# Self- and cross-attention of a decoder layer: row maxima for four heads at a time, and the scores of two heads in separate halves of TensorE's rows

## The chip, the cores and the metric

The kernel runs on one core of a Trainium2 chip (trn2). The metric is device time in microseconds, the median of three executions: 1087.91 us before the change (1082.69 to 1088.86).

## The reference, cut to what matters

One decoder layer over x (2 x 1024 x 256, float32) and a context (2 x 77 x 256): a causal self-attention block with a recurrent scan and an MLP behind it, a cross-attention block, and a tree-routed feed-forward. Both attentions have 16 heads of 16 features. What the change touches:

```python
# self-attention, b=2, h=16, 1024 queries and keys, 16 features
scores = jnp.einsum('bhqd,bhkd->bhqk', q, k) / np.sqrt(HD).astype(np.float32)
scores = jnp.where(causal[None, None], -jnp.inf, scores)
attn_w = jax.nn.softmax(scores, axis=-1)
attn = jnp.einsum('bhqk,bhkd->bhqd', attn_w, v)
...
# cross-attention: the same over 77 keys, without the mask
scores = jnp.einsum('bhsd,bhtd->bhst', qh, kh) / jnp.sqrt(jnp.float32(D_K))
attn = jax.nn.softmax(scores, axis=-1)
```

## The kernel before

The layer is one program with an instruction stream written out by hand for each engine. Semaphores set the order between engines; within an engine the order is that of the code. The attention stages, which run from about 89 to 398 us (self) and from about 726 to 826 us (cross), are the same code with an object `A` (`SA` or `XA`).

**Quads.** The 16 heads x 2 batches are taken as 8 quads of four heads, n = 2 * it + qd, on two sets of buffers (qd = 0, 1). q and k of a quad are first written to DRAM, each as a rounded high part and a low part, and are loaded back by SP in the two layouts below.

**First pass, the maxima (PE `unit`, DVE `maximum`).** It uses q1 and k1, the high parts alone: four heads of 16 features are interleaved on 64 partitions (the other 64 are zero), and k1 holds for each head a copy in which the other heads' rows are zero. One unit is one head h, one tile i of 128 queries and up to 512 keys: a matmul of 128, 256, 384 or 512 columns into bank 5, 6 or 7 of PSUM (`nbanks` is 3). Where it reaches the diagonal, a second matmul of 128 columns adds the mask: ident_b (128 x 128) as the weights, causal_b as the columns. A quad has 48 units, 32 of them with a mask. DVE reduces each to one column of part_max (128 x 64), `gather` reduces that to row_max (128 x 32), PE transposes it (`turn`), DVE negates it into neg_max, and SP copies neg_max by DMA into q2 (`load_max`).

**Second pass, the probabilities (PE `scores`, ACT, POOL, PE `weigh`).** The scores are computed transposed, with keys as the output's partitions, and the query's negated maximum is added by the matmul itself: q2 and k2 hold three parts of each head's 16 features (R2 = 48 rows) and one row for the maximum. Two heads (j = 0, 1) share one q2 of 98 rows: head 0 on rows 0 to 47, head 1 on rows 48 to 95, the maxima on rows 96 and 97. k2 has one copy for each j in which the other head's 48 rows are zero, so each of the two matmuls runs over all rows of the array. A quad has 12 steps (a chunk c of 512 queries by a tile kt of 128 keys; at the diagonal 512, 384, 256 or 128 columns), each with two pairs p. One ACT instruction takes exp of a pair (128 x 1024), POOL zeroes the upper triangle of the diagonal block, and `weigh` multiplies by the values with four heads side by side in 32 columns of the array each, 8 matmuls in plain float32.

**Order on PE.** While it computes quad n's second pass, PE works ahead on quad n + 1's first pass (and the first 8 units of n + 2). In a step: `scores` p = 0, a quarter of the step's units, `scores` p = 1, a quarter, `weigh` of the step before, then the other half of the units. `A.plan` deals the units to steps by their columns. A unit waits until DVE has reduced the unit three before it (`s1_free`), `scores` waits for the exp that read its banks (`prob_ready`), `weigh` for exp and for POOL's mask. In the last quad there are no units left.

**Order on SP.** For each quad: `load_first` (q1, k1), `load_second` (q2, k2: three DMAs), stores and loads of results, `load_max`. During the first quad's units, `qk_beside` puts the projections of the second batch between them (one at every third unit from u = 6), and SP stores those.

**POOL at the start (`preset_keys`, `preset_rest`).** It writes the zeros and ones of k1, k2, q1, q2, once for each attention stage, with a tensor_scalar of 10.8 us on two rows twice for SA.

## Time and profile before

| what | before |
|---|---|
| median of 3 (us) | 1087.91 (1082.69 to 1088.86) |
| the profiled execution's own time (us) | 1090.43 |
| its span, first to last instruction (us) | 1088.9 |
| busy share: PE / DVE / ACT / POOL | 85% / 59% / 43% / 16% |
| instructions | 13085 |
| first pass: L1395 matmuls / L1398 masks / L1051 reduces | 384 / 256 / 384 |
| second pass, self: L1421 / L1439 matmuls, L758 exps | 384 / 768 / 192 |
| mean granted TensorE clock, share of full | 0.914 |
| HBM traffic over the span | 72 GB/s |

Times are microseconds from the first instruction of one profiled execution, unless marked ns. A PE matmul's time runs from its start to the modelled end of its pipeline, so matmuls that follow one another overlap: the pace of a stream is read from their starts, or from the time of a merged group. PEld is the load of a matmul's weights. "PEclk" is the granted TensorE clock as a share of 2.4 GHz. A line number names a line of the kernel before; where the printed code is a helper, the tile's names tell whose instruction it is.

### The profile page before, as it was taken

To read this page: it belongs to the slowest core of one execution; us is meant where nothing else is said; L and a number is where in the kernel's file an instruction comes from. 1 tells how busy PE (TensorE), PEld (TensorE's weight loads), DVE (VectorE), ACT (ScalarE), POOL (GpSimd) and SP (SyncE) were. 2 spreads that over 40 slices of the span, in tenths; PEclk is the share of its full clock that TensorE was granted. 3 is DMA by queue.
4 is the path that set the end of the run, shared out by engine and by line. 5 is a ranking of instruction groups with operands and counts; after the bars stand their busy time and mean duration, and the time that the engine had idled before them with its cause. 6 is when DMAs were issued, how large, how long until landed. Compare 5 with 4: busy or idle time off the path is not lost. (4 is left out here: it accounts for less than half of the span.)

```text
span 1088.9 us, 13085 instructions
## 1 busy us (share of the span) xinstructions
PE 930.5 (85%) x4200; PEld 569.7 (52%) x4200; DVE 639.8 (59%) x1023; ACT 465.8 (43%) x683; POOL 170.0 (16%) x200
## 2 busy tenths in 40 slices
PE   5767699999999986999997899954673899999996
PEld 3553455555555433544445778622230477777774
DVE  4635677777777415277785644433331667777775
ACT  2301055555655662466654455412542243333332
POOL 7910012211122212000011400200010001111110
PEclk9887699999999997899998899975876889999998
DMA  3056534323444115100000000055854000000002
GB/s 119 19 201 179 192 78 108 98 67 75 105 108 98 33 59 198 70 1 0 1 0 23 2 1 1 2 180 161 234 154 130 21 0 20 20 19 19 19 20 77
DMA packets 34329, 79.34 MB, mean 73 GB/s; under 512 B 8121, under 2 KB 11193, under 8 KB 33897
## 3 DMA queue, kind: packets, MB, share of 16 engines
q1 hardware_dynamic: 29288, 70.64, 22.1%
q10 hardware_dynamic: 2688, 5.33, 1.4%
q0 software_dynamic: 2304, 2.76, 1.0%
q8 instruction: 27, 0.44, 0.2%
q14 instruction: 22, 0.17, 0.1%
HBM read 48.34 MB, written 30.10 MB: 72 GB/s over the span
## 5 line engine op out<-in xcount | busy, mean ns | idle before, releaser
L1051 DVE TENSOR_REDUCE part_max<-psum 128x1 f32<-128x512 f32 (+3 forms) x384 | 197.5, 553 | 85.5 <-PE psum L1398 54.9
L758 ACT ACTIVATE prob<-psum 128x1024 f32<-128x1024 f32 (+1 forms) x192 | 145.8, 809 | 107.9 <-PE psum L1421 107.8
L1395 PE MATMUL psum<-k,q 128*128 128x512 f32 (+3 forms) x384 | 141.3, 418 | 22.4 <-DMA k<-k 16.7
L1395 PEld LDWEIGHTS psum<-k,q 128*128 128x128 f32 x384 | 73.8, 202 | 88.3 <-DVE part_max L1051 60.5
L1421 PE MATMUL psum<-q,k 128*128 128x512 f32 (+3 forms) x384 | 105.7, 373 | 7.5 <-DMA q<-neg_max 6.2
L652 POOL TENSOR_SCALAR_AFFINE_SELECT prob<-prob 128x256 f32<-128x256 f32 x128 | 52.1, 416 | 256.9 <-ACT prob L758 255.7
L915 ACT ACTIVATE silu<-psum,wt 128x512 f32<-128x512 f32 x64 | 40.5, 685 | 117.2 <-DVE decide L1294 86.0
L1439 PE MATMUL psum<-prob,vq 128*32 128x512 f32 (+3 forms) x768 | 81.8, 498 | 2.0 <-POOL prob L652 1.6
L1421 PEld LDWEIGHTS psum<-q,k 128*128 128x128 f32 x384 | 61.4, 196 | 21.0 <-ACT prob L758 9.9
L1305 DVE TENSOR_TENSOR masked_lo<-masked,masked_hi 128x1024 fp32r<-128x1024 f32 x32 | 47.0, 1468 | 38.5 <-ACT masked_hi L923 38.5
L328 PE MATMUL psum<-masked_hi,wt_hi 128*128 128x512 f32 x128 | 56.1, 438 | 6.6 <-DVE res L1310 6.4
L1398 PE MATMUL psum<-causal_b,ident_b 128*128 128x128 bf16 x256 | 60.7, 239 | 0.0
L1525 PE MATMUL psum<-act_u,wx 128*128 128x512 f32 x128 | 55.8, 593 | 0.0
L1525 PE MATMUL psum<-nrm,wx 128*128 128x512 f32 x128 | 55.6, 593 | 0.0
L1401 PE MATMUL psum<-xk,xq 128*128 128x312 f32 (+1 forms) x64 | 24.8, 438 | 34.3 <-DVE row_max L1054 17.9
L758 ACT ACTIVATE xprob<-psum 77x1024 f32<-77x1024 f32 x32 | 31.6, 1014 | 49.2 <-PE psum L1421 49.1
L328 PE MATMUL psum<-tree_hi,wt_hi 128*128 128x512 f32 x128 | 51.3, 401 | 0.2 <-ACT silu L915 0.2
L330 PE MATMUL psum<-masked_hi,wt_lo 128*128 128x512 f32 x128 | 51.2, 400 | 0.0
L329 PE MATMUL psum<-masked_lo,wt_hi 128*128 128x512 f32 x128 | 51.2, 400 | 0.0
L329 PE MATMUL psum<-nrm_lo,wt_hi 128*128 128x512 f32 x128 | 50.9, 398 | 0.0
L330 PE MATMUL psum<-tree_hi,wt_lo 128*128 128x512 f32 x128 | 50.8, 397 | 0.0
L1054 DVE TENSOR_REDUCE row_max<-psum 128x4 f32<-128x312 f32 x64 | 28.9, 477 | 32.5 <-PE psum L1401 31.6
(165 smaller groups left out, 1656.4 us busy)
## 6 DMA issues: line engine op xcount, KB each, us to landing
q<-q SPq DMA_DIRECT2D x8, 768.0 KB, 6.3
k<-k SPq DMA_DIRECT2D x16, 384.0 KB, 8.4
xq<-xq SPq DMA_DIRECT2D x8, 768.0 KB, 5.6
wt<-in_wt SPq DMA_DIRECT2D x8, 513.0 KB, 3.7
q<-part_hi SPq DMA_DIRECT2D x16, 256.0 KB
k<-part_hi SPq DMA_DIRECT2D x16, 256.0 KB
o<-stage SPq DMA_DIRECT2D x8, 512.0 KB, 7.7
xq<-xpart_hi SPq DMA_DIRECT2D x16, 256.0 KB
```

The source lines that it names most:

```text
L328: pe.matmul(out, rounded(w_hi), rounded(x_hi), start=start, stop=False)
L329: pe.matmul(out, rounded(w_hi), rounded(x_lo), start=False, stop=False)
L330: return pe.matmul(out, rounded(w_lo), rounded(x_hi), start=False, stop=stop)
L652: pool.affine_select(out=blk, in_=blk, compare_op=ALU.is_ge, fill=0.0, base=0, pattern=[[0, 2], [1, P]], channel_multiplier=-1)\
L758: act.activation(A.prob[0:A.keys, s % 2, p, :, q0:CH], psum[0:A.keys, 2 * p:2 * p + 2, q0:CH], ACT.Exp, scale=SCALE)\
L1051: dve.tensor_reduce(part_max[:, at:at + 1], psum[:, 5 + u % A.nbanks, 0:nk], AX_X, ALU.max)\
L1305: dve.tensor_tensor(rounded(masked_lo[:, st.buf]), masked[:, st.buf], masked_hi[:, st.buf], ALU.subtract)\
L1395: mm = pe.matmul(psum[:, 5 + u % A.nbanks, 0:nk], A.q1[:, qd, i * P:(i + 1) * P], A.k1[:, qd, h, k0:k0 + nk], start=True, stop=not diag)
L1398: mm = pe.matmul(psum[:, 5 + u % A.nbanks, nk - P:nk], ident_b[:], causal_b[:], start=False, stop=True)
L1421: mm = pe.matmul(psum[0:A.keys, 2 * p + j, q0:CH], A.k2[:, qd, p, j, kt * P:kt * P + A.keys], A.q2[:, qd, p, c * CH + q0:(c + 1) * CH], st ...
L1439: mm = pe.matmul(psum[32 * h:32 * h + 32, 4, q0:CH], A.vq[:, qd, kt, h, :], A.prob[:, s % 2, h // 2, h % 2, q0:CH], start=first, stop=last)
L1525: mm = pe.matmul(bank(2 * c + m), wx01[:, k, m * P:(m + 1) * P], state(n)[:, k, cols_of(c)], start=False, stop=k == 1, skip_group_check=True)
```

## The change

- **Units.** A unit is now a tile i of queries by one tile kt of 128 keys for all four heads: always 4 x 128 = 512 columns, 36 units a quad, over 64 rows instead of 128. The 8 diagonal units get their mask by two matmuls of 256 columns (causal_b, now 64 rows x 2, as the weights; a 64 x 64 identity repeated for four heads as the columns). DVE reduces 512 columns to four maxima in one instruction, as it did in cross-attention; part_max grows to 32 x 8 columns, which `gather` reduces.
- **Scores.** The heads of a pair lie on partitions 0 to 48 and 64 to 112: 48 rows of features and one of the maximum (q2) or of ones (k2) each. The matmul of head j reads those 49 rows alone. k2 has lost its copies with zeros. q2 is loaded by two DMAs instead of one (`ld2_n` 16 * 4).
- **Presets.** The zeros of q1 and q2, the full zeroing of k2 and POOL's tensor_scalar are gone.
- `weigh`, exp, POOL's mask, the order on PE and the number of banks stay as they are. Both attention stages take part in the scores' and the presets' change; the new units are self-attention's.

```diff
+HALF = P // 2
-        ident_b = sb("ident_b", [P, P], BF16)
-        causal_b = sb("causal_b", [P, P], BF16)
+        ident_b = sb("ident_b", [HALF, 1, HALF], BF16)
+        causal_b = sb("causal_b", [HALF, 2, P], BF16)
-        part_max = sb("part_max", [P, 64])
+        part_max = sb("part_max", [P, 32, SEQ // P])
-        k2 = sb("k2", [P, 2, 2, 2, SEQ], F32R, s_self)
+        k2 = sb("k2", [P, 2, 2, SEQ], F32R, s_self)
...
-        self_units = [(h, i, kh * CH, min(CH, (i + 1) * P - kh * CH), i // TPC == kh)
-                      for h in range(4) for i in range(SEQ // P) for kh in range(i // TPC + 1)]
+        self_units = [(kt, i, kt * P, CH, i == kt) for i in range(SEQ // P) for kt in range(i + 1)]
...
-                sp.dma_start(A.q2[0:2 * R2, qd, :, :].bitcast(F32),
-                             A.q3[4 * qd:4 * qd + 4, :, :, at].rearrange("(p j) r d t -> (j r d) p t", p=2))\
-                    .then_inc(A.ld2[qd], 16)
                 for j in range(2):
-                    sp.dma_start(A.k2[R2 * j:R2 * j + R2, qd, :, j, :].bitcast(F32),
+                    sp.dma_start(A.q2[HALF * j:HALF * j + R2, qd, :, :].bitcast(F32),
+                                 A.q3[4 * qd + j:4 * qd + 4:2, :, :, at].rearrange("p r d t -> (r d) p t"))\
+                        .then_inc(A.ld2[qd], 16)
+                for j in range(2):
+                    sp.dma_start(A.k2[HALF * j:HALF * j + R2, qd, :, :].bitcast(F32),
...
-                sp.dma_start(A.q2[2 * R2:2 * R2 + 2, qd, :, :].bitcast(F32), neg_max[:, qd, :].bitcast(F32))\
+                sp.dma_start(A.q2[R2:P:HALF, qd, :, :].bitcast(F32), neg_max[:, qd, :].bitcast(F32))\
...
-                pool.memset(k1[:].bitcast(F32), 0.0)
-                pool.memset(k2[:].bitcast(F32), 0.0).then_inc(zeros_set, 1)
-                pool.memset(k2[2 * R2:2 * R2 + 2].bitcast(F32), 1.0).then_inc(ones_set, 1)
-                for j in range(2):
-                    row = k2[2 * R2:2 * R2 + 2, :, :, j, :].rearrange("r b p n -> r (b p) n")
-                    pool.tensor_scalar(row, row.bitcast(F32), ident[2 * R2:2 * R2 + 2, 2 * R2 + j:2 * R2 + j + 1],
-                                       None, ALU.mult).then_inc(ones_set, 1)
+                pool.memset(k1[0:HALF].bitcast(F32), 0.0).then_inc(ones_set, 1)
+                pool.memset(k2[32:HALF].bitcast(F32), 1.0)
+                pool.memset(k2[HALF + 32:P].bitcast(F32), 1.0).then_inc(zeros_set, 1)
...
-                        dve.tensor_reduce(part_max[:, at:at + 1], psum[:, 5 + u % A.nbanks, 0:nk], AX_X, ALU.max)\
+                        dve.tensor_reduce(part_max[:].rearrange("q (j p i) k -> q p j i k", j=2, p=2)[:, :, :, i, kt],
+                                          heads, AX_X, ALU.max).then_inc(A.s1_free, 1)
...
-                        mm = pe.matmul(psum[:, 5 + u % A.nbanks, 0:nk], A.q1[:, qd, i * P:(i + 1) * P],
-                                       A.k1[:, qd, h, k0:k0 + nk], start=True, stop=not diag)
+                        mm = pe.matmul(heads, A.q1[0:HALF, qd, i * P:(i + 1) * P], A.k1[0:HALF, qd, :, k0:k0 + P],
+                                       start=True, stop=not diag)
                         if diag:
-                            mm = pe.matmul(psum[:, 5 + u % A.nbanks, nk - P:nk], ident_b[:], causal_b[:], start=False, stop=True)
+                            for r in range(2):
+                                mm = pe.matmul(heads[:, :, r * HALF:(r + 1) * HALF], causal_b[:, r, :],
+                                               ident_b[:].to_broadcast([HALF, 4, HALF]), start=False, stop=r == 1)
...
-                                       A.k2[:, qd, p, j, kt * P:kt * P + A.keys],
-                                       A.q2[:, qd, p, c * CH + q0:(c + 1) * CH], start=True, stop=True)
+                                       A.k2[HALF * j:HALF * j + R2 + 1, qd, p, kt * P:kt * P + A.keys],
+                                       A.q2[HALF * j:HALF * j + R2 + 1, qd, p, c * CH + q0:(c + 1) * CH],
+                                       start=True, stop=True)
```

## Rows read from the trace of the kernel before

**Rows 1.** Stretches: length, each engine's busy time, PEclk, DMA share, GB/s

```profile
89.00:134.80 45.80, 37.19 (x127) 20.53 (x128) 33.58 (x66) 5.50 (x8) 0.00 (x0) 0.76 0.63 200
202.60:236.60 34.00, 33.00 (x225) 18.56 (x221) 25.06 (x51) 18.67 (x26) 6.79 (x17) 1.00 0.35 87
...
372.90:398.20 25.30, 22.37 (x153) 9.23 (x153) 2.57 (x2) 18.91 (x26) 7.65 (x17) 1.00 0.17 54
754.00:780.00 26.00, 24.38 (x120) 11.13 (x120) 14.44 (x33) 18.80 (x26) 0.83 (x1) 0.92 0.81 204
```

**Rows 2.** Timeline: DVE's gather of two quads in a row (start, duration)

```profile
335.48 0.22 DVE L1063 TENSOR_REDUCE row_max<-part_max 128x32 f32<-128x64 f32 x1
...
369.30 0.22 DVE L1063 TENSOR_REDUCE row_max<-part_max 128x32 f32<-128x64 f32 x1
```

**Rows 3.** Waits, 134 to 373 us: total, times, longest

```profile
ACT prob L758 <- PE psum L1421: 102.0, 83, 2.7
...
DVE part_max L1051 <- PE psum L1398: 35.9, 70, 0.9
```

**Rows 4.** Timeline of one full step in steady state

```profile
217.19 0.71 PE L1421 MATMUL psum<-q,k 128*128 128x512 f32 x2
...
218.25 1.44 DVE L1051 TENSOR_REDUCE part_max<-psum 128x1 f32<-128x512 f32 x2 [0.27 <-PE psum L1398]
...
218.56 0.40 PE L1395 MATMUL psum<-k,q 128*128 128x512 f32 x1
...
218.89 1.07 PE L1439 MATMUL psum<-prob,vq 128*32 128x512 f32 x8
219.88 0.19 PEld L1395 LDWEIGHTS psum<-k,q 128*128 128x128 f32 x1 [0.84 <-DVE part_max L1051]
...
220.56 0.48 PE L1421 MATMUL psum<-q,k 128*128 128x512 f32 x1
```

**Rows 5.** Chain that ended last: 512-column rounded matmuls at either clock

```profile
1045.72 0.24 PE psum L329
...
1077.12 0.43 PE psum L329
```

**Rows 6.** Timeline of PE in groups of four scores matmuls

```profile
371.22 0.67 PE L1421 MATMUL psum<-q,k 128*128 128x128 f32 x4
...
386.96 1.19 PE L1421 MATMUL psum<-q,k 128*128 128x512 f32 x4
...
389.08 1.38 PE L1421 MATMUL psum<-q,k 128*128 128x512 f32 x4
```

**Rows 7.** Instruction groups by form: count, busy us, mean ns, idle before

```profile
L1051 DVE TENSOR_REDUCE part_max<-psum 128x1 f32<-128x512 f32 x192 | 128.6, 687 | 39.1 <-PE psum L1395 27.4 <-PE psum L1398 10.2
...
L1421 PE MATMUL psum<-q,k 128*128 128x512 f32 x192 | 65.9, 428 | 6.9 <-DMA q<-neg_max 6.2 <-ACT prob L758 0.5 <-issue 0.3
...
L1054 DVE TENSOR_REDUCE row_max<-psum 128x4 f32<-128x312 f32 x64 | 28.9, 477 | 32.5 <-PE psum L1401 31.6
...
L1421 PE MATMUL psum<-q,k 128*128 128x128 f32 x64 | 9.8, 276 | 0.0
...
L1063 DVE TENSOR_REDUCE row_max<-part_max 128x32 f32<-128x64 f32 x8 | 1.8, 220 | 0.8
```

**Rows 8.** Timeline: the first quad's maxima and the start of its second pass

```profile
125.21 1.08 SPq L506 DMA_DIRECT2D q<-neg_max  x1
...
134.81 1.19 PE L1421 MATMUL psum<-q,k 128*128 128x512 f32 x2 [6.17 <-DMA q<-neg_max]
...
135.01 1.28 ACT L758 ACT_TABLE_LOAD   x1 [22.67 <-DMA k<-part_hi]
```

**Rows 9.** Timeline: plain float32 projections, two instructions to a matmul

```profile
44.32 14.16 PE L1355 MATMUL psum<-nrm,w 128*128 128x512 f32 x32
```

**Rows 10.** Timeline: POOL's last preset and the first load behind it

```profile
53.98 3.51 POOL L614 MEMSET q<- 32x4096 f32 x1
...
84.05 0.63 SPq L479 DMA_DIRECT2D q<-q  x1
```

More of the change, by code:

```diff
@@ L266, in __init__ @@
                 self.ld1_n = 16 * 5 if causal else 16
-                self.ld2_n = 16 * 3
+                self.ld2_n = 16 * 4
                 self.nsteps = len(self.steps)
@@ L619, in _ @@
             pool.wait_ge(c_in, 16 * 4)
-            pool.tensor_copy(ident_b[:], ident[:])
+            pool.tensor_copy(ident_b[:, 0, :], ident[0:HALF, 0:HALF])
             pool.tensor_copy(causal_b[:], caus_f[:])
             preset_keys(k1, k2, 1)
-            preset_rest(q1, q2, vq, sums, 1)
+            preset_rest(vq, sums, 1)
             def attention(A, vals, ready):
@@ L688, in _ @@
             pool.wait_ge(xk_st, 16 * 3 * KT)
-            preset_rest(xq1, xq2, xvq, xsums, 2, xprob)
+            preset_rest(xvq, xsums, 2, xprob)
             attention(XA, xvals, (xv_done, 2))
@@ L697, in _ @@
         def _(act):
-            for t, n in ((vec[:], "vec"), (ident[:], "ident"), (caus_f[:], "causal"), (mean_w[:], "mean_w")):
+            for t, n in ((vec[:], "vec"), (ident[:], "ident"), (mean_w[:], "mean_w")):
                 act.dma_start(t, a[n]).then_inc(c_in, 16)
+            act.dma_start(caus_f[:], a["causal"].rearrange("(h r) n -> r h n", h=2)).then_inc(c_in, 16)
             act.dma_start(vbias[:], a["vbias"]).then_inc(w_in3, 16)
@@ L1043, in maximum @@
                     n = 2 * it + qd
-                    h, i, k0, nk, diag = A.units[u]
-                    row = 16 * (h % 2) + 8 * (h // 2) + i
+                    kt, i, k0, nk, diag = A.units[u]
+                    heads = psum[:, 5 + u % A.nbanks, 0:nk].rearrange("q (p j k) -> q p j k", p=2, j=2)
                     dve.wait_ge(A.s1_ps, n * A.nunits + u + 1)
@@ L1049, in maximum @@
                     if A.causal:
-                        at = 2 * row + k0 // CH
-                        dve.tensor_reduce(part_max[:, at:at + 1], psum[:, 5 + u % A.nbanks, 0:nk], AX_X, ALU.max)\
-                            .then_inc(A.s1_free, 1)
+                        dve.tensor_reduce(part_max[:].rearrange("q (j p i) k -> q p j i k", j=2, p=2)[:, :, :, i, kt],
+                                          heads, AX_X, ALU.max).then_inc(A.s1_free, 1)
                     else:
                         dve.tensor_reduce(row_max[:].rearrange("q (j p i) -> q p j i", j=2, p=2)[:, :, :, i],
-                                          psum[:, 5 + u % A.nbanks, 0:nk].rearrange("q (p j k) -> q p j k", p=2, j=2),
-                                          AX_X, ALU.max).then_inc(A.s1_free, 1)
+                                          heads, AX_X, ALU.max).then_inc(A.s1_free, 1)
                 def gather(it, qd):
@@ L1387, in unit @@
                     n = 2 * it + qd
-                    h, i, k0, nk, diag = A.units[u]
+                    kt, i, k0, nk, diag = A.units[u]
+                    heads = psum[:, 5 + u % A.nbanks, 0:nk].rearrange("q (h k) -> q h k", h=4)
                     if u == 0:
@@ L1394, in unit @@
                     if A.causal:
-                        mm = pe.matmul(psum[:, 5 + u % A.nbanks, 0:nk], A.q1[:, qd, i * P:(i + 1) * P],
-                                       A.k1[:, qd, h, k0:k0 + nk], start=True, stop=not diag)
+                        mm = pe.matmul(heads, A.q1[0:HALF, qd, i * P:(i + 1) * P], A.k1[0:HALF, qd, :, k0:k0 + P],
+                                       start=True, stop=not diag)
                         if diag:
-                            mm = pe.matmul(psum[:, 5 + u % A.nbanks, nk - P:nk], ident_b[:], causal_b[:], start=False, stop=True)
+                            for r in range(2):
+                                mm = pe.matmul(heads[:, :, r * HALF:(r + 1) * HALF], causal_b[:, r, :],
+                                               ident_b[:].to_broadcast([HALF, 4, HALF]), start=False, stop=r == 1)
                     else:
                         pe.sem_inc(passed, 1)
-                        mm = pe.matmul(psum[:, 5 + u % A.nbanks, 0:nk].rearrange("q (h k) -> q h k", h=4),
-                                       A.q1[:, qd, i * P:(i + 1) * P], A.k1[:, qd, :, bass.ds(it * CTXP, CTXP)],
+                        mm = pe.matmul(heads,
+                                       A.q1[0:HALF, qd, i * P:(i + 1) * P], A.k1[0:HALF, qd, :, bass.ds(it * CTXP, CTXP)],
                                        start=True, stop=True)
@@ L1691 @@
         "ident": np.eye(P, dtype=np.float32),
-        "causal": np.where(k <= q, 0.0, LOW).astype(np.float32),
+        "causal": np.where(q <= k, 0.0, LOW).astype(np.float32),
         "mean_w": np.full((P, P), 1.0 / D, np.float32),
```

20 lines of the change are left out of this document (8 added, 12 removed).

## The prediction

> **What bounds the kernel now.** I read the page's busy shares first, which say only that PE leads with 85% over a program of many stages, and then the table of stretches, one line to a quad of self-attention. In steady state a quad's second pass lasts 34.0 us, with PE marked busy for 33.0, DVE for 25.1 and ACT for 18.7, all at the full clock [rows 1]. The gathers of neighbouring quads stand 33.8 us apart [rows 2]. Seven quads carry units for later quads; the eighth has none left and takes 25.3 us [rows 1]. These seven are where this change acts, 7 x 34 = 238 us.
>
> Busy PE is not proof, since ends of matmuls are modelled. So I added up PE's own pace. A rounded 512-column matmul follows the next every 0.24 us [rows 5]; four of 128 columns take 0.67 us of which one's own 0.276 is latency, so (0.67 - 0.28) / 3 = 0.13 us each [rows 6, 7]; 384 and 256 columns I put between them at 0.20 and 0.17. One `weigh` of 512 columns holds PE from 218.89 to 219.88, 0.99 us [rows 4]. A quad has, for the scores, 24 matmuls of 512 columns and 8 each of 384, 256 and 128: 24 x 0.24 + 8 x 0.50 = 9.8 us. Its 48 units have the same mixture of columns: 9.8 us. 32 masks of 128 columns at 0.13 are 4.2. The 12 `weigh` are six full ones, 5.9, and two each at three quarters, a half and a quarter of that, 3.0: 8.9. Together 32.7 of the 34.0 us. PE's instruction stream is the bound; DVE and ACT wait for it. The waits agree: ACT stood 102 us for scores and DVE 36 us for masked units, over seven quads [rows 3]. In one full step (217.19 to 220.56, 3.37 us) DVE had two units of work, 1.44 us, and then stood until PE was through `weigh` [rows 4].
>
> **The units.** Columns stay 18,432 a quad, and the masks' 4,096. What goes is small instructions: 36 units x 0.24 = 8.6 us and 16 masks of 256 columns x 0.17 = 2.7, together 11.3 instead of 14.0. That is 2.7 us of PE per quad. From below: if masks in fact hid behind the loads of weights and cost only their columns (4,096 at 0.24 / 512 = 1.9 us before and after), the gain is 9.8 - 8.6 = 1.2 us. Half the rows make a matmul neither shorter nor longer in this sum, since its price goes by columns.
>
> DVE gets 36 reduces of 512 columns. The old ones took 687 ns [rows 7]; the form with four outputs exists in cross-attention, 477 ns for 312 columns, and 200 more at the slope of these two rows, (687 - 477) / 200 = 1.05 ns, meet at 687 ns. So four outputs cost nothing, and 36 x 0.687 = 24.7 us. The gather reads 256 columns instead of 64: 192 x 1.05 ns = 0.20 us on top of 0.22 [rows 7], in the chain gather, `turn`, negate, `load_max`, where it delays a DMA needed some microseconds later. With negate and the reciprocal DVE needs 24.7 + 1.0 = 25.7 us a quad, as now.
>
> **The scores in two halves.** No row of before shows two matmuls in two row halves. Bounds: if they take turns, a pair of 512 columns costs 0.48 us as now; if they run together, 0.24. The nearest row is `weigh`, which puts four heads in four column groups: its eight float32 matmuls take 0.99 us, while such float32 instructions alone follow one another every 14.16 / 32 = 0.44 us [rows 4, 9], so eight in turn would be 3.5 us. The array does work on separate parts at the same time here. I take the near end, with a little for the second head's weights, which go through one load path: 0.28 us for a pair of 512 columns, 0.25, 0.22 and 0.20 for the shorter. 12 x 0.28 + 4 x 0.67 = 6.1 us instead of 9.8: 3.7 us of PE a quad (best case 24 pairs at single price, 4.9; worst 0).
>
> The Trainium skill (TensorE: Matmul & The Clock Gate, section on packing small matmuls) has matmuls in different row groups start about 4 ns apart; by that the pair costs the single price and the gain is the best case. No trace here shows it.
>
> **What the quad becomes.** PE: 34.0 - 2.7 - 3.7 = 27.6 us. DVE at 25.7 is then nearly as long, and the two are tied by three banks: PE may be three units ahead, 3 x 0.687 = 2.06 us, and between units come a `weigh` (0.99) and up to two pairs. That covers most gaps, not all, and each unit's result takes some 0.4 us to arrive (0.40 for one in [rows 4]). I let DVE stand 0.1 us for each of 36 units: 25.7 + 3.6 = 29.3 us, between the floor of 27.6 and the 31.3 of the rival below. Gain 4.7 x 7 = 32.9 us.
>
> **The last quad.** There a full step is 2.12 us (386.96 to 389.08) [rows 6] and ACT's two exps are about 1.94 of it. The scores' gain of 0.4 a step is cut by ACT to about 0.2 to 0.3: 6 full steps x 0.25 and 6 short ones x 0.15 give 2.4 us (bounds 0 and 3.7).
>
> **Before steady state.** From 89 to 124 us the first quad's units run between the projections. PE's second pass starts at 134.81, when the row of maxima has landed that was issued at 125.21 behind the stores of q and k; ACT is free at 135.01 when the last of these stores lands [rows 8]. DVE is busy for 33.6 us there [rows 1]. Every third unit is now 0.69 long instead of 0.51 on average, so the projections spread out by about 0.5 us each, up to 3 us at the last of them, but the DMA queue behind them carries 200 GB/s and is still draining 10 us later. 12 fewer units take the time back for the maxima. I take 0, between -2 and +3 us.
>
> **Presets and DMAs.** POOL ends its presets at 57.5 us and the first load that needs them is issued at 84.05 [rows 10]. Work of up to 30 us goes and gains nothing, since SP's stores of q and k cover it. Without that cover it would have been worth the lot. The same holds in front of cross-attention. One more DMA a quad costs SP about 0.6 us of issue, where SP waits for maxima anyway; bytes are the same.
>
> **Cross-attention.** Its steady part has PE 24.4 of 26.0 us busy, ACT 18.8 and DMA engines at 81% [rows 1]. 32 pairs could save 0.2 each, 6.4 us; most goes to ACT and the loads. I take 1 us (0 to 4).
>
> **Sum.** 32.9 + 2.4 + 0 + 1 = 36.3 us. The span becomes 1088.9 - 36.3 = 1052.6, the profiled execution's own time (1090.43, 1.5 above its span) 1054.1; the median before is 2.5 below that own time, so the same gain gives 1087.9 - 36.3 = 1051.6. I say 1052 us. Its own range is 1040 to 1062: the two PE terms at their better bounds with DVE's standing halved, or the units at their lower bound.
>
> **Rivals.**
>
> *DVE takes over.* PE runs ahead, but DVE's idle time falls only from 8.9 us (34.0 - 25.1) to 6 because units still come in bunches after `weigh`: quad 25.3 + 6 = 31.3, gain 2.7 x 7 + 3 = 22 us, 1066 us. For it: DVE already has 74% of the quad, and a reduce never gets shorter here. Against: in this trace DVE waits for PE, not the reverse. The Trainium skill (TensorEngine Tiling, PSUM Bottleneck) warns of just this: tiling speeds up TensorE but not the emptying of PSUM. Its rule has no figure to add.
>
> *The halves take turns.* Only the units gain, 2.7 x 7 and nothing else, some of it blurred: 1070 us.
>
> *The halves cost a drain.* PE went from a unit at 218.56 (0.24 long) to `weigh` at 218.89: 0.09 us lost at a change of shape [rows 4]. If each pair paid that once or twice, 24 pairs cost 2.2 to 4.3 us a quad against the 2.7 of the units: 1084 us, no change to measure. The skill (TensorEngine Tiling, Key Properties) says that a change of mode drains and a change of tile does not; by it units, masks and scores now share one mode, and the count of changes around `weigh` is as before.
>
> *The clock falls; the slower side.* With 64 and 49 rows in use and PE waiting more, the granted clock could drop in self-attention, where it is 1.00 now. It is 0.76 on average from 89 to 134.8 us, where PE waits for DVE and DMA [rows 1]. At half clock a 512-column matmul paces 0.43 [rows 5] instead of 0.24; a quad's 27.6 us of PE holds some 21 us of streaming, which would double. The gain of 4.7 us is used up when 4.7 / 21 = 22% of the streaming is at half clock. At half of it a quad takes 29.3 + 10.5 = 39.8: 5.8 x 7 = 41 us slower, 1129 us. Against: in the last quad, where PE is 22.4 of 25.3 us busy with gaps of its own, the clock stayed 1.00.
>
> **Chances.** 1052: 0.60. DVE takes over: 0.14. Turns: 0.09. Drain: 0.06. Clock: 0.11, of which 0.10 slower. 0.5% is 5.4 us, about what a measurement of this kernel can tell from no change. Faster 0.84, same 0.06, slower 0.10. The range reaches from the likeliest case's lower end to the two middle rivals: 1036 to 1076 us.
>
> **What would show it.** Second matmul of a pair starting 0.1 us or less after the first, not 0.24. Gathers about 29 us apart. 288 reduces near 687 ns. DVE's waits for units below 20 us in all. Full steps of the last quad near 2.0 us. PEclk 1.00 from 145 to 390 us. It is wrong if pairs start 0.24 apart, if PEclk shows falls there, or if gathers stand over 31 us apart.

## The result, and the profile after

The kernel after takes **1125.01 us** (1117.51 to 1128.56, four runs) against 1085.66 for the kernel before in the same series: ratio **1.034**, interval 1.030 to 1.038. It is slower, by 3.4%. The forecast was 1052 us. Here and in the experiments, medians count all runs, while a ratio and its interval leave out runs more than 1.5% above the fastest of the same kernel, which show a lower granted clock.

The span of its profiled execution is 1123.2 us, 34.3 longer than before. First, where the 34.3 us arose, by four landmarks. The first quad's gather starts at 127.20 us, 3.3 later than before (123.92). From the first gather to the eighth pass 264.2 us instead of 245.4: 18.8 more. From there to the end of the last self-attention `weigh` it is 33.1 instead of 28.9 us: 4.2 more. Between the first and last exp of cross-attention lie 79 us instead of 72: 7 more. The rest comes to about 1 us in sum. None of these four parts became shorter.

The table of stretches, from each gather to the next (length; busy PE, PEld, DVE, ACT, POOL with their counts; PEclk; DMA share; GB/s):

```profile
127.20:172.28 45.08, 38.20 (x154) 18.09 (x154) 24.65 (x40) 16.84 (x20) 3.64 (x10) 0.55 0.38 97
172.28:201.09 28.81, 27.76 (x198) 13.02 (x197) 23.34 (x38) 18.91 (x26) 6.86 (x18) 1.00 0.46 102
201.09:236.46 35.37, 30.45 (x197) 13.91 (x196) 23.94 (x39) 19.02 (x26) 7.34 (x18) 0.89 0.38 84
236.46:285.11 48.65, 48.65 (x205) 21.49 (x197) 24.84 (x38) 19.33 (x26) 6.89 (x17) 0.50 0.32 72
285.11:328.93 43.82, 43.82 (x206) 19.70 (x198) 24.71 (x40) 19.33 (x26) 6.59 (x17) 0.59 0.32 67
328.93:357.46 28.53, 27.73 (x198) 13.02 (x197) 23.35 (x39) 18.91 (x26) 6.91 (x18) 1.00 0.49 104
```

These lines answer to [rows 1, 2]. Two quads ran at full clock throughout: 28.8 and 28.5 us, PE busy for 27.8 and 27.7 of them. The forecast had 29.3 and 27.6. One quad ran at half clock throughout: 48.65 us, PE busy for all of it, DVE and ACT busy for nearly as long as in the fast ones (24.8 and 19.3 us against 23.3 and 18.9). The work in the lines is the same: as many matmuls, reduces and exps. So at half clock a gain of 5 us a quad is a loss of 15. Over the seven quads together (127.20 to 391.42) PEclk is 0.74, against 0.97 from 123.92 to 369.30 in the kernel before: about half of the time is at half clock.

The groups of the page (mean of one, then the idle time before them):

```profile
L1044 DVE TENSOR_REDUCE part_max<-psum 128x4 f32<-128x512 f32 x288 | 185.3, 686 | 112.6 <-PE psum L1388 72.1
L1388 PE MATMUL psum<-k,q 64*128 64x512 f32 x288 | 144.2, 543 | 28.0 <-DMA k<-k 16.8
L1416 PE MATMUL psum<-q,k 49*128 49x512 f32 (+3 forms) x384 | 119.1, 473 | 8.2 <-ACTq L739 6.3
```

288 reduces of four maxima at 686 ns, as forecast. Means of PE (543, 473 ns) mix both clocks.

The timeline of PE at full clock shows the halves at work:

```profile
219.35 0.50 PE L1416 MATMUL psum<-q,k 49*128 49x512 f32 x2
...
221.01 0.49 PE L1388 MATMUL psum<-k,q 64*128 64x512 f32 x1
221.02 0.49 PE L1416 MATMUL psum<-q,k 49*128 49x512 f32 x1
221.34 0.39 PE L1388 MATMUL psum<-k,q 64*128 64x512 f32 x1
221.57 0.59 PE L1416 MATMUL psum<-q,k 49*128 49x512 f32 x2
221.81 0.39 PE L1388 MATMUL psum<-k,q 64*128 64x512 f32 x1
222.04 0.40 PE L1416 MATMUL psum<-q,k 49*128 49x512 f32 x1
222.29 0.49 PE L1388 MATMUL psum<-k,q 64*128 64x512 f32 x1
```

Three units and four score matmuls take 1.28 us, from 221.01 to 222.29; one after another they would take 7 x 0.24 = 1.68. A score matmul, the second head's by its place in the order, begins at 221.02, 0.01 us after a unit in the lower half. The two of a pair take 0.50 us together at 219.35, where one alone takes 0.39 to 0.50, and 0.59 at 221.57; in the kernel before, two took 0.71 [rows 4]. So the sign that I had named for the halves came, and the second head's matmul also runs beside a unit.

Where does the clock fall? PE around 228 us, then DVE, then PEclk in stretches of 4 us:

```profile
224.51 0.40 PE L1416 MATMUL psum<-q,k 49*128 49x512 f32 x1
228.83 0.76 PE L1388 MATMUL psum<-k,q 64*128 64x512 f32 x1 [3.92 <-DVE part_max L1044]
228.92 1.09 PE L1416 MATMUL psum<-q,k 49*128 49x512 f32 x2
```

```profile
221.54 1.89 DVE L1044 TENSOR_REDUCE part_max<-psum 128x4 f32<-128x512 f32 x3 [0.58 <-PE psum L1388]
227.67 0.55 DVE L1072 RECIPROCAL recip<-sums 128x64 f32<-128x64 f32 x1 [4.25 <-DMA sums<-o]
228.14 3.02 DVE L1044 TENSOR_REDUCE part_max<-psum 128x4 f32<-128x512 f32 x5
```

```profile
224.00:228.00 4.00, 0.91 (x6) 0.42 (x4) 0.33 (x1) 1.02 (x1) 0.00 (x0) 1.00 0.18 57
228.00:232.00 4.00, 3.17 (x12) 0.96 (x12) 3.17 (x6) 1.02 (x1) 0.00 (x0) 0.61 0.02 4
232.00:236.00 4.00, 4.00 (x18) 2.18 (x18) 2.33 (x4) 1.94 (x2) 0.41 (x1) 0.50 0.00 0
316.00:320.00 4.00, 4.00 (x17) 1.49 (x14) 1.98 (x3) 2.10 (x3) 0.00 (x0) 0.50 0.01 1
320.00:324.00 4.00, 4.00 (x24) 2.25 (x23) 3.27 (x6) 1.94 (x2) 0.00 (x0) 0.87 0.00 0
```

Read them in turn. DVE runs a reciprocal in the middle of every second quad, over sums that come by DMA (issued at 222.20, usable at 227.6). The same DMA took as long before (issued at 217.55, the reciprocal at 223.35), but DVE, in slower quads, reached the reciprocal only 1.1 us too early; now it is 4.25. The row of before:

```profile
223.35 0.55 DVE L1080 RECIPROCAL recip<-sums 128x64 f32<-128x64 f32 x1 [1.10 <-DMA sums<-o]
```

Behind the reciprocal stand the reduces, PE has filled its three banks and stands 3.92 us. Then the clock is half, from 229 to about 321 us, 92 us in which PE is busy all the time. At 383 us it happens again (DVE waits 3.77, PE 3.45), and the clock is half from 386 to 406 us.

That suggests two theories. **Stall** ("gap" in the texts below): the wait at the reciprocal lets the clock fall. **Rows** ("theory 1" in some of them): with matmuls over 64 and 49 rows the clock falls more easily and returns late, whatever starts it. A third suspect, unseen in this trace, is a cost of **changing** between matmuls over all rows and over a half; the experiments that mix them speak on it.

### The profile page after: what moved, and what is told of

Its sections match the earlier page's. It is cut to its first block and busy times, and to the rows that moved or that the text cites. A ratio compares the mean times of both kernels' runs of the same rounds, so it can differ in the third digit from the quotient of the medians.

```text
span 1123.2 us, 12434 instructions
## 1 busy us (share of the span) xinstructions
PE 956.6 (85%) x3963; PEld 545.7 (49%) x3976; DVE 625.5 (56%) x927; ACT 465.2 (41%) x683; POOL 129.3 (12%) x192
## 5 line engine op out<-in xcount | busy, mean ns | idle before, releaser
L1044 DVE TENSOR_REDUCE part_max<-psum 128x4 f32<-128x512 f32 x288 | 185.3, 686 | 112.6 <-PE psum L1388 72.1
L1388 PE MATMUL psum<-k,q 64*128 64x512 f32 x288 | 144.2, 543 | 28.0 <-DMA k<-k 16.8
L1416 PE MATMUL psum<-q,k 49*128 49x512 f32 (+3 forms) x384 | 119.1, 473 | 8.2 <-ACTq L739 6.3
L1388 PEld LDWEIGHTS psum<-k,q 64*128 64x128 f32 x288 | 62.8, 236 | 118.2 <-DVE part_max L1044 61.1
L1435 PE MATMUL psum<-prob,vq 128*32 128x512 f32 (+3 forms) x768 | 105.6, 630 | 3.2 <-POOL prob L645 3.1
L1416 PEld LDWEIGHTS psum<-q,k 49*128 49x128 f32 x384 | 62.3, 234 | 33.9 <-ACT prob L752 18.2
L1396 PE MATMUL psum<-xk,xq 64*128 64x312 f32 (+1 forms) x64 | 30.4, 527 | 26.7 <-DMA xq<-xq 17.2
L1047 DVE TENSOR_REDUCE row_max<-psum 128x4 f32<-128x312 f32 x64 | 28.8, 477 | 42.3 <-PE psum L1396 42.2
L1314 PE MATMUL psum<-wide,mean_w 128*128 128x512 f32 x32 | 23.0, 809 | 24.2 <-DVE wide L931 24.2
```

Source lines behind the costliest of these rows:

```text
L1044: dve.tensor_reduce(part_max[:].rearrange("q (j p i) k -> q p j i k", j=2, p=2)[:, :, :, i, kt], heads, AX_X, ALU.max).then_inc(A.s1_free, 1)
L1388: mm = pe.matmul(heads, A.q1[0:HALF, qd, i * P:(i + 1) * P], A.k1[0:HALF, qd, :, k0:k0 + P], start=True, stop=not diag)
L1416: mm = pe.matmul(psum[0:A.keys, 2 * p + j, q0:CH], A.k2[HALF * j:HALF * j + R2 + 1, qd, p, kt * P:kt * P + A.keys], A.q2[HALF * j:HALF * j ...
L1435: mm = pe.matmul(psum[32 * h:32 * h + 32, 4, q0:CH], A.vq[:, qd, kt, h, :], A.prob[:, s % 2, h // 2, h % 2, q0:CH], start=first, stop=last)
```

## The experiments

Ratios are to the kernel before on the same chip, whose medians lay between 1087 and 1093 us.

**1. The stall taken away.** The kernel after, and DVE's reciprocal where its sums have landed:

```diff
-if k == len(todo) // 2 and qd == A.recip_qd and more:
+if k == (len(todo) - 3 if A.causal else len(todo) // 2) and qd == A.recip_qd and more:
```

> The changed kernel with one edit: in self-attention DVE's reciprocal of the row sums (it waits for a DMA) stands three reduces before the end of its quad instead of in the middle. In the changed kernel PE stood 3.9 us there at 224.9 us, and the granted clock was 0.50 from 230 to about 320 us. Theory 'gap': the stall alone makes the clock fall, rows in use do not matter. Then without the stall the clock stays 1.00 from the second quad on, all quads take about 28.5 us and the time is about 1065 us. Theory 'rows': matmuls over 64 and 49 rows let the clock fall or keep it low by themselves. Then it still falls somewhere in self-attention and the time stays above 1095 us. Both expect the first quad (138 to 173 us in the changed kernel) to stay slow.

Measured: 1078.76 us (1064.07 to 1096.80), and in a second series (r1b_late_again) 1091.11 (1074.27 to 1103.92).

> The same kernel as r1_late_recip once more (the kernel after with the reciprocal three steps before the end), as the neighbour of the next ones on the same chip. First result: 1078.8 us, with quads of 28.6 us at full clock and one long fall with no stall ahead of it. Expected: 1065 to 1095 again, quads 28.5 at full clock, and falls at other places than the first time, since no stall sets them.

The ratio of the second series is 0.989 (0.982 to 0.996); the first has none. Of the ten runs of both, the middle is 1082 us: some 40 less than the kernel after. Neither theory's total came, 1065 us or above 1095. The wait is gone; four quads in a row take 28.6 to 28.9 us. But a long fall remains. In PE's timeline and the stretches of this kernel:

```profile
285.95 0.50 PE L1388 MATMUL psum<-k,q 64*128 64x512 f32 x1 [0.56 <-DVE neg_max L1062]
```

```profile
285.00:287.00 2.00, 1.44 (x11) 0.51 (x13) 1.17 (x4) 1.51 (x2) 0.48 (x2) 0.99 0.00 0
287.00:289.00 2.00, 2.00 (x12) 0.70 (x5) 0.41 (x1) 0.00 (x0) 0.33 (x1) 0.50 0.33 76
```

PE had idled 0.56 us, as it does once in each quad (0.57 to 0.66 us in the four quads before, where the clock stayed full), and the clock was half from 287 to 317 us. In the second series's profile it fell at 287 as well, not at another place as expected, and returned only at about 366. The stall is a trigger, not the only one, and a long stretch at half clock comes without it.

**2. Which half of the change.** Units widened to all 128 rows with zeros, their masks too, scores in halves (the first line of the edit is shown); and units over 64 rows, scores over all rows as before.

```diff
-A.q1[0:HALF, qd, i * P:(i + 1) * P], A.k1[0:HALF, qd, :, k0:k0 + P]
+A.q1[:, qd, i * P:(i + 1) * P], A.k1[:, qd, :, k0:k0 + P]
```

> The changed kernel with its units and masks over all 128 rows (rows 64 to 127 of q1 and k1 are zeros, the mask is one matmul of 512 columns with a 128-row identity); the scores stay in halves and the reciprocal's stall stays. Theory 'rows': the clock may fall at the stall but comes back within about 6 us, as at the start of the kernel before (134.8 to 140.7 us), and the time is about 1065 us, even 1055. Theory 'gap' with rows of no importance: the clock falls at the same stall and stays low as long as in the changed kernel: about 1125 us.

Measured: 1103.21 us, ratio 1.010 (1.006 to 1.013).

> The kernel before with the new units alone (four heads at once, 64 rows, masks over 64 rows), the scores over 98 rows as before. No two matmuls run at once in it but weigh's. Both theories give a quad of 31 to 32 us at full clock, so about 1070 us if the clock holds. Theory 'rows' expects the clock to suffer less than in the changed kernel, since half of the row matmuls are full again, but to come back later than 140.7 us in the first quad. Theory 'gap' expects a stall for the reciprocal of 1 to 3 us, too short, and a clock as in the kernel before.

Measured: 1179.59 us, ratio 1.079 (1.074 to 1.083). One full quad of each at full clock, first the full units, then the full scores, and behind them one quad of the latter at half clock:

```profile
163.88:197.88 34.00, 33.10 (x193) 12.82 (x189) 24.43 (x39) 19.26 (x26) 6.92 (x18) 1.00 0.40 87
```

```profile
338.68:376.35 37.67, 37.25 (x201) 15.95 (x197) 25.24 (x40) 19.90 (x26) 6.95 (x18) 1.00 0.31 78
186.69:252.30 65.61, 65.61 (x205) 25.75 (x197) 24.87 (x39) 20.11 (x26) 7.05 (x17) 0.50 0.18 45
```

Each half of the change, joined to full-row matmuls of the other kind, takes 34 and 37.7 us where both halves together take 28.6. That can't be the clock, which is 1.00 in these lines. With full units a fall at 230 us, behind a DVE wait of 2.55 us, was over in some 7 us, as "rows" has it, but the total of 1103 us fits neither theory (1065 or 1125). With full scores the clock was half from 121 to 277 us, from 138 on with PE busy all the time. That is longer than in the kernel after, although more of the matmuls read all rows here; "rows" had expected the opposite, and "stall" a clock as in the kernel before. So the count of rows does not by itself say how long a fall lasts.

**3. All over all rows.** The kernel before with units of four heads, but over 128 rows; scores as before. And the kernel before with the scores in halves alone, units as before.

> The kernel before with the four-head units alone, and these over all 128 rows (zeros in the upper 64, as before), masks one matmul of 512 columns; scores as before over 98 rows. No matmul works in half of the rows. Theory 1 (the rows in use decide how soon the clock comes back): the clock falls at the end of the first pass and where PE stands, but is back within 3 to 6 us, as in the kernel before with the early reciprocal; quads 31.3 us at full clock (34.0 less the 2.7 predicted for units), total about 1069, range 1062 to 1080. Rival (the unit's shape or order, not the rows, brings the falls): long stretches at half clock as in the kernel after, quads of 45 us, total 1095 or more. Rival 2 (the predicted 2.7 us for units is not there): quads 34, total 1088.

Measured: **1070.72 us** (1068.89 to 1084.84), ratio 0.988 (0.982 to 0.994), as theory 1 of the text had it (1062 to 1080).

> The kernel before with the scores in two halves of 49 rows alone; the 48 units stay over all 128 rows. If changes between matmuls over all rows and matmuls in a half cost time, as the two mixed kernels so far say: quads 34.0 + 2.7 = 36 to 37 us, total 1100 to 1110. If they cost nothing: quads 34.0 - 3.7 = 30.3 us, total near 1062 unless the clock falls. PEclk in either case back within about 6 us after a fall, since the units use all rows.

Measured: 1124.41 us, ratio 1.032 (1.027 to 1.037), slower even than expected. Stretches, the first kernel's (two quads) and the second's:

```profile
193.44:225.34 31.90, 31.23 (x193) 16.50 (x189) 24.38 (x39) 19.12 (x26) 6.92 (x17) 1.00 0.37 92
225.34:257.08 31.74, 31.16 (x193) 16.57 (x189) 24.02 (x39) 19.13 (x26) 6.92 (x17) 1.00 0.44 110
```

```profile
183.43:219.63 36.20, 35.52 (x229) 16.81 (x225) 25.45 (x51) 19.32 (x27) 6.93 (x18) 1.00 0.37 81
```

With the four-head units alone the quad is 31.9 instead of 33.9, and PEclk is 1.00 from 144 to 392 us. With the halves alone it is 36.2 at the same clock. Why, PE's timeline shows, of the halves alone and then of all rows:

```profile
243.06 0.50 PE L1416 MATMUL psum<-q,k 49*128 49x512 f32 x2
243.49 0.50 PE L1390 MATMUL psum<-k,q 128*128 128x512 f32 x1
243.92 0.51 PE L1416 MATMUL psum<-q,k 49*128 49x512 f32 x2
```

```profile
242.68 0.63 PE L1422 MATMUL psum<-q,k 128*128 128x512 f32 x2
243.15 0.39 PE L1395 MATMUL psum<-k,q 128*128 128x512 f32 x1
243.37 0.62 PE L1422 MATMUL psum<-q,k 128*128 128x512 f32 x2
```

A unit between two pairs holds PE for 0.43 us (243.49 to 243.92) instead of 0.22. A pair and a unit together take 0.86 us when mixed, 0.69 all over full rows; the pair in halves should have saved 0.2 of the 0.69. So each change between a half and the full array costs about 0.2 us here.

Over whole quads it is a little less. By the way the printed code deals units to steps (`A.plan`, `share`), a quad has 24 changes from one kind of matmul to another (over all rows, over a half, `weigh`) when units and scores are alike, 63 in the halves alone, and 57 in the two kernels of experiment 2. The halves alone should take 33.9 - 3.3 = 30.6 us and take 36.2: 5.6 us for 39 changes more, 0.14 each. Full scores beside new units take 37.7 instead of 31.9, full units beside halves 34.0 instead of 28.6: 5.8 and 5.4 us for 33, 0.18 and 0.16 each.

My expectation for the clock was wrong: here too it stayed at half for 65 us, from 116 to 181, from 136 on with PE busy, though the units use all rows.

**4. Fewer changes.** Both pairs of a step behind one another, the units behind them:

```diff
-                        ahead(it, qd, A.share(s, 0), more)
                         scores(it, qd, s, 1)
+                        ahead(it, qd, A.share(s, 0), more)
```

> The halves alone (s1_halves_only, 36.2 us a quad at full clock) with both pairs of a step issued behind one another, and the units between them moved behind: 24 fewer changes a quad between matmuls over all rows and matmuls in a half. Theory (each such change costs 0.12 to 0.2 us): a quad becomes 3 to 4.5 us shorter, 31.7 to 33.2, total 1095 to 1103. Rival (what s1 lost is something else, such as a longer load of weights): 36 us as there; or DVE and ACT stand longer for their work and the quad is longer.

Measured: 1106.18 us (ratio 1.014, 1.008 to 1.020), 18 less.

```profile
235.98:269.74 33.76, 33.03 (x229) 15.90 (x225) 25.02 (x51) 19.13 (x27) 6.92 (x17) 1.00 0.45 104
```

Three quads take 33.8 instead of 36.2 us; three others at mostly full clock are 1 to 4 us longer than that. The saving of 2.4 us is below the 3 to 4.5 of the text. But the text counts 24 changes fewer, and by the deal of the units it is 16 (63 to 47), since in 4 of the 12 steps no unit stands between the pairs. 2.4 / 16 is 0.15 us each, in line with experiment 3. The price of a change is 0.14 to 0.2 us in all four kernels that mix.

**5. The reciprocal in the kernel over all rows.**

> As the one with four-head units over all rows, and DVE's reciprocal three steps before the end of a quad instead of in its middle. Theory 1: DVE's wait for the sums goes (1 to 2 us a quad in four of the quads), and with it short falls of the clock: 5 to 10 us less than its neighbour, about 1062. Rival: the wait costs nothing with quads of 31 us, total the same within 3 us.

Measured: 1078.14 us (ratio 0.989, against 0.988), the same within the spread, so the rival holds. From the first gather to the eighth its profile has 230.3 us instead of 232.8, so the wait costs 2 to 3 us at most; its first gather is 10.2 us later, for a reason ahead of the attention that this edit doesn't touch.

**6. Rows, one thing at a time.** The kernel of experiment 1, and score matmuls that read all 64 rows of their half (15 more, zeros in q2):

```diff
-A.q2[HALF * j:HALF * j + R2 + 1, qd, p, c * CH + q0:(c + 1) * CH]
+A.q2[HALF * j:HALF * (j + 1), qd, p, c * CH + q0:(c + 1) * CH]
```

> The kernel above with one thing changed: each score matmul reads all 64 rows of its half (rows 49 to 63 of q2 are zero) instead of 49, so that a pair works in 128 rows, not 98, at the same columns. Theory 1 (rows in use hold the clock, zeros or not): falls are fewer or shorter, 5 to 20 us less than its neighbour, while a quad at full clock stays at 28.5. Rival (the rows' number does not matter to the clock; it is the pace of matmuls): no difference beyond 5 us.

Measured: **1075.31 us** (1071.41 to 1080.31, six runs), ratio 0.985 (0.980 to 0.990), against its neighbour's 1091.11 (1074.27 to 1103.92) and 0.989 (0.982 to 0.996). The two ratios can't be told apart; what the rows change is that the long runs are gone. From 170 to 342 us six quads in a row take 28.5 to 28.7 us, with PEclk 1.00 until 348. Two of them:

```profile
256.22:284.89 28.67, 27.77 (x198) 12.99 (x197) 23.39 (x39) 18.91 (x26) 7.00 (x18) 1.00 0.58 121
284.89:313.40 28.51, 27.71 (x198) 13.01 (x197) 23.66 (x40) 18.92 (x26) 6.95 (x18) 1.00 0.51 103
```

The same columns, the same pace, only more rows: the fall at 287 us is not there. It is in both profiles with 49 rows and in none of the four with 64 rows and a late reciprocal (this one and the three of experiment 8), though PE idles there as before (0.57 us). And the stall left in:

> The kernel after with one thing changed: score matmuls read all 64 rows of their half; the reciprocal stays in the middle, so PE's 4 us stalls stay. If the rows alone were the cause: PEclk back within 10 us of each stall and no other falls, total 1085 to 1095 (stalls of 4 us and short falls, against 1075 without the stall). If the stall is the trigger and 64 rows hold the clock but cannot bring it back quickly: falls of 30 us and more after each stall, as in the kernel after, total 1105 to 1125.

Measured: 1101.53 us (1085.49 to 1114.62, twelve runs), ratio 1.003 (0.998 to 1.008). In its profile, a run of 1085.8 us, PE stood 5.05, 4.96 and 2.90 us at the three reciprocals, and the clock was full again 4 to 6 us after PE went on; in the kernel after that took 92 us. But the longer runs show lower clocks (0.856 against 0.887), so it wasn't always so, and the median lies between the two totals expected. The two-by-two of stall and rows, in us and as ratios: 1125 (1.034) and 1101.5 (1.003) with the stall, 1082 (0.989) and 1075 (0.985) without. The stall counts for 26 to 43 us. The 15 rows count for 24 us with the stall; the 7 us without it are not clear of the noise.

**7. Units in both halves.** Even units in the lower half, odd ones in the upper, everything loaded twice.

> The kernel after with the late reciprocal, and q1, k1 and the mask in both halves: even units work in rows 0 to 63, odd ones in rows 64 to 127, so that two neighbouring units can run at the same time. Q1 and k1 are loaded twice (0.5 MB more a quad, one DMA more). PE's time for units and masks falls by up to 11.3 / 2 = 5.6 us a quad, DVE's 25.7 us bound the quad: 26 to 28 us at full clock instead of 28.6. Theory 1 (rows in use hold the clock): it is at half clock for less time than the same kernel with all units in one half (some 105 us of 128 to 430), total 1045 to 1065. Rival (it is PE's share of idle time that lets the clock fall, whatever the rows): PE idles more, so the clock is lower for longer, total above 1079.

> Units alternating between the halves (as r6_alt_units, 27.8 us a quad at full clock, 1090.7 us in all) and score matmuls over all 64 rows of their halves. Theory 1: the clock holds longer than in r6_alt_units, total 1060 to 1080. Rival: 1085 to 1095 as there.

Measured: 1090.68 us (ratio 1.002) and 1091.48 (1.001). Quads at full clock are 27.8 us, but two of each kernel's take 38. Stretches from the second kernel:

```profile
268.00:272.00 4.00, 0.00 (x0) 0.00 (x0) 0.00 (x0) 0.00 (x0) 0.00 (x0) 0.77 0.68 166
336.00:340.00 4.00, 0.00 (x0) 0.00 (x0) 0.00 (x0) 0.00 (x0) 0.00 (x0) 0.50 1.04 169
```

In those quads PE stands 4 to 8 us ahead of a second pass (7.95 us until 274.24 and 8.05 until 340.62 here; 4.22 and 7.75 in the first kernel), the first time for the DMA of the row of maxima, and the clock is half for 10 to 20 us around it; once, in the first kernel, it fell some 7 us ahead of the wait. Also the first gather comes at 136 to 138 us instead of 120 to 130, behind twice the loads: PE waits 30.2 us for k at the start instead of 15.8. For both kernels the total went with the rival, which had PE idle more; the length of the falls went with theory 1. So these kernels decide nothing between the two.

**8. Work over all rows in the wait.** Nearly all kernels are at half clock ahead of the second pass. The one of experiment 6 stays so until about 165 us. Into PE's 6 us wait at 131:

```diff
+                for _ in range(12 if A.causal else 0):
+                    pe.matmul(psum[:, 4, :].rearrange("q (h k) -> q h k", h=4), ident[:],
+                              ident[:].rearrange("p (o k) -> p o k", o=1).to_broadcast([P, 4, P]), start=True, stop=True)
                 over_iterations(pe, quad, True)
```

> The kernel r8_64_rows (late reciprocal, 64 rows for each score matmul) with 12 matmuls of 512 float32 columns over all 128 rows (identity by identity, into a bank that nobody reads then) in the 6 us in which PE waits for the row of maxima ahead of the second pass. Theory 1 (work over all rows brings the clock back): it rises during or soon after them, the first quad takes 29 to 35 us instead of 45, total 1058 to 1066 against 1075. Rival (the clock comes back after a time of its own, whatever PE does): first quad 45 us or, as the 12 delay the second pass at half clock, 48; total 1075 to 1080.

> The kernel r10_warm with its 12 matmuls in front of the second pass over rows 0 to 63 only; same columns, same places. Theory 1 (rows in use count): the clock does not rise during them, the block takes 20 us instead of 12.6, or it rises late; first quad at half clock for a good part, total 1075 to 1085. Rival (dense streaming is enough, whatever the rows): as r10_warm, clock back 5 us into the block, total 1061 to 1068.

Measured: 1064.40 us (1060.85 to 1067.79), ratio 0.976 (0.971 to 0.981), over all rows; and 1080.36 us (ratio 0.993) with the same 12 over 64 rows. Stretches of the first and of the second:

```profile
130.70:133.00 2.30, 2.30 (x4) 1.17 (x4) 1.16 (x2) 0.00 (x0) 0.00 (x0) 0.50 0.52 203
133.00:135.00 2.00, 2.00 (x3) 0.67 (x2) 0.00 (x0) 0.00 (x0) 0.00 (x0) 0.52 0.53 202
135.00:139.00 4.00, 4.00 (x11) 1.80 (x10) 0.00 (x0) 1.24 (x1) 0.00 (x0) 1.00 0.25 75
```

```profile
130.80:135.00 4.20, 4.20 (x6) 1.66 (x5) 1.32 (x3) 0.00 (x0) 0.00 (x0) 0.50 0.53 204
135.00:150.00 15.00, 15.00 (x20) 5.99 (x19) 0.00 (x0) 1.28 (x1) 0.00 (x0) 0.50 0.74 152
150.00:165.00 15.00, 15.00 (x60) 7.40 (x59) 7.03 (x11) 5.20 (x8) 3.21 (x8) 0.50 0.07 10
```

This is the clearest pair. PE is busy without a gap in both, with the same instructions over the same columns. Over 128 rows the clock is full 4 us into the block, which begins at 130.7. Over 64 rows it is half through the block's 20 us and 20 us beyond, until 172. In this pair the rows decide. The two kernels' runs don't overlap either (1060.85 to 1067.79, and 1074.57 to 1088.03). The first quad takes 39.8 us with the 12 and not the 29 to 35 expected, since the block itself holds PE for 12.6; over 64 rows it takes 56.0.

Six instead of twelve:

> The kernel r10_warm with 6 matmuls instead of 12. They last about 8 us at mostly half clock, until 138.5, when the second pass can start (137.5 without them). If the clock has risen by then (134.5 in r10_warm) and stays: 4 to 5 us less than r10_warm, 1059 to 1061. Rival: the shorter block is not enough and the clock falls back or never rises: first quad 45 us, total about 1075.

Measured: **1058.66 us** (1050.61 to 1077.94), ratio **0.971** (0.968 to 0.974), where 1059 to 1061 us was expected; it is the fastest kernel of the study, 6% under the kernel after and 3% under the one before. In the kernel over all rows the same 12 changed nothing to measure:

> The kernel r4_both_full (all matmuls over 128 rows, quads 31.9 us) with the same 12 matmuls in the wait ahead of the second pass. Theory 1: the first quad takes 32 to 35 us instead of 41.6, total 1061 to 1066 against 1070.7. Rival: no change, or 2 to 4 us slower by the delay.

Measured: 1074.16 us, ratio 0.985 (0.979 to 0.991); in its profile the clock had come back at 124 us, ahead of the block at 125.1.

**9. The stall in the kernel before.** Its reciprocal moved ahead, so that DVE waits as long as in the kernel after.

> The kernel before with one edit: DVE's reciprocal stands at 19 of 48 reduces of its quad instead of 24, so that it waits about 4 to 5 us for its DMA in three quads, as in the changed kernel, while every matmul keeps its full rows. Theory 'gap' without rows: the clock falls at each stall and stays low for a quad or two as in the changed kernel: 30 to 60 us slower. Theory 'rows' (a gap trips the clock, full-row matmuls bring it back soon): three times a stall of 3 us on PE and some 6 us at half clock, 10 to 20 us slower.

Measured: 1103.52 us, ratio 1.012 (1.006 to 1.018), as "rows" had it (10 to 20 us). Around the first of the three stalls:

```profile
220.00:224.00 4.00, 0.08 (x1) 0.08 (x1) 1.23 (x4) 0.00 (x0) 0.00 (x0) 1.00 0.10 28
224.00:228.00 4.00, 4.00 (x17) 2.30 (x17) 2.24 (x5) 2.05 (x2) 0.00 (x0) 0.57 0.00 0
228.00:232.00 4.00, 4.00 (x27) 1.96 (x23) 2.97 (x6) 1.94 (x2) 0.00 (x0) 1.00 0.00 0
```

Three DVE waits of 4.0 to 4.5 us, in which PE stood 4.04, 3.82 and 3.54; quads with one take 39 to 40 us instead of 34, so about 6 us each: the stall itself and 3 to 7 us at half clock. The kernel after stood as long, 3.92 us, and there it left the rest of that quad, the next and most of the one after at half clock.

## Why the prediction was wrong

**The step that failed** is the clock in the sum. "What the quad becomes" prices all seven quads at full clock, 29.3 us each, and no term stands for a fall; the fall appears only as the rival "The clock falls", at a chance of 0.11. What the runs showed in its place: 28.6 us a quad at full clock, 48.65 at half clock, and PEclk 0.74 over the seven, which makes 37.7 us on average (264.2 / 7). A stall of 3.9 us begins the long fall, and with few rows in use it lasts 92 us instead of 3 to 7. I argued against the rival that in the last quad, where PE has gaps of its own, the clock stayed 1.00. All matmuls of that trace read 128 rows; it could say nothing of 49 and 64. The row of my own that pointed the other way, 0.76 on average from 89 to 134.8 us, I laid to waits.

The rival's mechanism, few rows and PE waiting, was right. That its totals are so near, 39.8 us a quad and 1129 us against 37.7 and 1125, is in part luck: it took half of the streaming at half clock as an example, for which no row gave a share. By the mean PEclk of 0.74 about half of the time was at half clock, an estimate, which is about a third of the work, and the first quad's wait for its maxima is in the average as well.

**A step was missing:** what is late next on DVE. I asked of DVE only how long it is busy. Its reciprocal waits for a DMA that takes 5.5 to 5.8 us in a quad of either length; a shorter quad brings DVE there 3 us sooner. In the trace of before the row was there, a wait of 1.1 us.

**PE's two terms** were right in size. Units: 2.7 forecast, 2.0 measured (33.9 to 31.9 with units alone). Scores: 3.7 forecast, 3.3 measured (31.9 to 28.6). Prices by columns hold at full clock for 64 and 49 rows. But they can't be had one by one: by itself the halves term is a loss of 2.3 us a quad, for the changes between matmuls over all rows and over a half, and a quad with 64-row units and full-row scores is 3.8 us longer than before. At full clock the whole pays because units, masks and scores change together, as the text had it under the rival "The halves cost a drain", which stays beaten. The Trainium skill (TensorEngine Tiling (Array Packing), Key Properties) has a change of tiling mode drain TensorE. The traces agree that such a change costs time, 0.14 to 0.2 us here; that it is a drain, no row shows.

**The quad** at full clock: 29.3 forecast, 28.6 measured, by two errors that partly cancel. DVE is busy for 23.4 us and not 25.7, since reduces behind one another follow every 0.60 us (five in 3.02) and not every 0.687; and it stands 5.2 us and not 3.6, so its waits for units are well above the 20 us in all that I named as a sign. PE, busy for 27.7, stays the bound. "DVE takes over" and "the halves take turns" are beaten.

**Last quad:** forecast 2.4 less, measured 4.2 more; the clock, again, half from 386 to 406 us. **Before steady state:** forecast 0 (-2 to +3), measured +3.3 to the first gather and 4.2 more for the first quad (45.1 against 40.9). In both stretches the clock is half for longer than before: until 103 us instead of 93, and until 167 instead of 140. **Presets:** right; the first load is issued at 84.04 us as before. **Cross-attention:** forecast 1 less, measured 7 more. With halves in use there PEclk is 0.63 and 0.55 over its two halves of time, against 0.83 and 0.77 before, and the kernel of experiment 3 with cross-attention as before has 70.5 us between its first and last exp. All profiles with the halves there have 75 to 82 us. That the clock makes the difference is not shown: the kernel with full scores and 64-row units has 64 us at 0.71 and 0.52. A version with the halves in self-attention alone wasn't tried.

**What stays open:** why the clock falls where PE hardly stands, as at 287 us in experiment 1, twice at the same place; with more rows it was gone in four profiles, but what set it off isn't shown. And why it returned so late in the kernels that mix rows (half from 138 to 277 us and from 136 to 181 with PE busy), later than rows alone would have it.

## What to carry to other kernels

That the pace by columns stays the same does not make a cut in the rows free: the clock can stay low for longer, and at half clock a quad here took 1.7 times as long (48.65 / 28.6). Where operands must shrink, try the rows filled with zeros and full-row matmuls in PE's waits, both of which helped here, and measure the clock of every stretch. Change all matmuls that alternate, or none: mixing halves and the full array cost 0.14 to 0.2 us at each change. And when a loop becomes shorter, list every in-order instruction in it that waits for a DMA which doesn't become shorter with it.

## What the runs showed of the hardware that I had not expected

- The clock's return depends on rows in use: full 4 us into a block of full-row matmuls, still half after 40 us of unbroken work in which all but `weigh` read 64 rows, and after 90 us in the kernel after. Zeros in the rows count: with 15 zero rows more for each score matmul a fall of 30 and 79 us (287 to 317, 287 to 366) was gone.
- Changes between matmuls over 128 and over 64 or 49 rows cost 0.14 to 0.2 us each. Matmuls of different halves run beside one another: 0.01 us apart, four score matmuls and three units in 1.28 us.
- Kernels with few rows can scatter: 1064 to 1104 us for the one with the late reciprocal, where the one with 15 rows more has 1071 to 1080; with the stall left in, that one scatters too (1085 to 1115).
